# A decoder layer on one core: a third query ahead of the last quotients, half of one tile's scaling on VectorE, and the gate's second choice behind unit 4's scores

## The chip, the cores and the metric

The kernel runs on one core of one Trainium2 chip. The metric is the device time of one execution in microseconds (us). The engines are named as the profile names them: PE (TensorE, with its weight loads as PEld), DVE (VectorE), ACT (ScalarE), POOL (GpSimd) and SP (SyncE, which issues most transfers). SBUF is the on-chip memory, PSUM the accumulators, eight banks that the program calls `pb`.

## The reference

The input is `x`, 2 x 1024 tokens of 256 numbers, all float32. Three blocks are added to it in turn, each on its layer norm:

```
x = x + linear_attention(layernorm(x))      # k, q through elu+1, two decayed running sums, 16 heads, divided by q*running k
x = x + cross_attention(layernorm(x), ctx)  # 16 heads, 154 context rows per batch:
        att = softmax(where(mask, -inf, q k^T / 8 * side))
        out = (att v) Wo + bo
x = x + experts(layernorm(x))               # softmax gate over 8 experts, the best two per token,
        y = sum of the two experts' silu((x w1 + b1) * (x w3 + b3)) w2 + b2, weighted by their scores
        z = a shared expert of the same form; y + z is added
```

## The kernel before, in words

The 2048 tokens are 16 tiles of 128 tokens, four chunks `c` of four tiles, and eight units `u8` of two tiles. Each engine has its own program, written out by hand in one order; engines meet only in semaphores. A `Signal` is a semaphore with a list of events in order, `w.wait_ge(scaled.sem, scaled[t, hf])` waits for one of them.

The PSUM banks are given in rotation: `bank.take(key)` takes the next of the eight, `take_pair` two neighbours that one instruction of DVE will drain together (and it skips bank 7 when no pair fits). PE may fill a bank when its last user has drained it, `w.wait_ge(free[u.e], u.empty)`. So the order of the `take` calls on PE decides which earlier content each fill has to wait for.

First comes the linear attention, chunk by chunk. For chunk 3, PE makes the first queries of the cross attention for unit 0 (`queries(0, ...)`, L489, L498), the sum of the denominators (`densum`, L457), and after DVE's reciprocal (L1172) the spread quotients (`divided`, L468), which DVE multiplies in (L1180). The line `queries(0, range(4, 6))`, `divided(3)`, `queries(0, range(6, 8))` is L679 to L681.

Then the cross attention in units. For unit `u8` PE does the scores of two tiles in three groups of heads each (`scores`, L515), the queries of the next unit (L498), then for the unit before (`values`): the transposes of the softmax weights (`weights_turned`, L548; `hf` is a half of the 16 heads, `k` one bank of four transposes), the products with the values (`product`, L564 and L568), between them the place step of a gate (L623) in units 4 and 6 and the transposes of the next norm (`turned`, L394), then parts of the shared expert (L635, L647) and the combination with Wo (`combined`, L600, L612).

DVE, for each tile `t`: multiplies the scores with the side input (`scores`, L1206, three groups, draining the score banks), adds the mask (`mask`, L1217, two SBUF tensors), reduces to the maximum (`top`, L1224, L1227, L1230), takes the reciprocal of the softmax sum (`total`, L1236), and drains the value products (`product`, L1248) and the combination (`attended`, L1258). It also does norm statistics (`stats`, L1084, L1086), and for every second unit from 3 on the gate of a chunk: `logits`, then `gate`, in which each of some 20 steps (`step`, profiled as L1262) waits for the one before; after the first choice of an expert it calls `shared_act` (L1339), then makes the second choice. In unit 3 that is the gate of chunk 0. Its result, `gated[0]`, is used by PE's place step in unit 4.

ACT does the exponentials of the softmax (`exps`, L895), the evacuation of transposes and queries (L907, L886, L830) and the norms (L840). POOL multiplies the exponentials by the reciprocals into `wts` (`scale(t)`, L1668: for each half `hf` a product over the 26 context rows that exceed 128, L1680, 208 columns, and one over the first 128, L1682, 1024 columns), adds `boB` to x (`add_bo`, L1650, a product of 256 columns for each tile), computes the norms' roots (L1661 to L1666) and issues the scatters of tokens to their experts (L1686).

At the end come 36 slots of 128 rows, each with one expert's three matrices, and POOL adds their rows to the output in DRAM with indirect transfers (L1762).

Of the kernel before, what the change touches and what calls it, by code (L numbers as in the profile page):

```python
# [7 lines left out]
ALU = mybir.AluOpType  # L8
ACT = mybir.ActivationFunctionType
AX = mybir.AxisListType  # L10
# [5 lines left out]
P = 128  # L16
# [4 lines left out]
NT = N // P  # L21
NCH = 4
CT = 512
H = 16
# [147 lines left out]
def decoder(nc, A, xs, out):  # L172
    with ExitStack() as ctx:
# [6 lines left out]
        def signal(name, events):  # L180
            return Signal(sem(name), events)
# [166 lines left out]
        topped = signal("topped", [(t, hs, n) for t in range(NT) for hs in heads_of(t) for n in range(3)])  # L348
        raised = signal("raised", range(NT))
        summed = signal("summed", range(NT))  # L350
        scaled = signal("scaled", [(t, hf) for t in range(NT) for hf in range(2)])
        xbo = signal("xbo", range(NU))
        xsb = signal("xsb", range(NCH))
        gatexp = signal("gatexp", range(NCH))
# [26 lines left out]
        def _(e):  # L381
# [158 lines left out]
            def weights_turned(u8, hf, k):  # L540
                u = bank.take(("pT", u8, hf, k))
                w.wait_ge(free[u.e], u.empty)
                for i in range(2):
                    n = 2 * k + i
                    lo = P * (8 * hf + n) if n < 8 else 2048 + P * (2 * hf + n - 8)
                    for q in range(2):
                        w.wait_ge(scaled.sem, scaled[2 * u8 + q, hf])
                        ins = e.transpose(pb[:, u.i, (2 * i + q) * P:(2 * i + q + 1) * P], wts[q][:, lo:lo + P],  # L548
                                          ident[:, :])
                ins.then_inc(full[u.i], 1)  # L550
# [125 lines left out]
                    contents(b)  # L676
            queries(0, range(0, 4))
            densum(3)
            queries(0, range(4, 6))  # L679
            divided(3)  # L680
            queries(0, range(6, 8))  # L681
            scores(0)
            queries(1)
            mixed(3)
# [385 lines left out]
        def _(e):  # L1070
# [120 lines left out]
            def scores(t, groups=range(3)):  # L1191
                s = t % 2
                w.wait_ge(in_fs[s], 16 * (t // 2 + 1))
                if t < 3:
                    w.wait_ge(qkv.sem, qkv[3, 1])
                    d = bank["mix", 2 if t < 2 else 3, 1]
                    w.wait_ge(full[d.i], d.filled)
                else:
                    w.wait_ge(scaled.sem, scaled[t - 3, 1])
                for g in groups:  # L1200
                    lo, hi = TRIOS[g]
                    n = hi - lo
                    u, v = bank["s", t, g, 0], bank["s", t, g, 1]
                    w.wait_ge(full[u.i], u.filled)
                    w.wait_ge(full[v.i], v.filled)
                    e.tensor_tensor(  # L1206
                        att[t % 3][:, 2 * lo:2 * hi, :].rearrange("p (r h) k -> p r h k", r=2),
                        pb[:, u.i:u.i + 2, 0:n * SK].rearrange("p r (h k) -> p r h k", h=n),
                        fs[:, s, 2 * lo:2 * hi, :].rearrange("p (r h) k -> p r h k", r=2), ALU.mult
                    ).then_inc(free[u.i], 1)  # L1210
# [23 lines left out]
            def total(t):  # L1234
                w.wait_ge(raised.sem, raised[t])
                e.reciprocal(mx[:, t % 4, 3, :], mx[:, t % 4, 2, :]).then_inc(*summed.next(t))  # L1236

            def product(u8, hf):
                w.wait_ge(in_bv, 16)
# [29 lines left out]
            def gate(c, amid=None):  # L1269
                u = bank["gateT", c]  # L1270
                lg4 = pb[:, u.i, 0:P].rearrange("p (t n) -> p t n", t=4)[:, :, 0:NE]
                w.wait_ge(in_sm, 224)
                w.wait_ge(to_xs, 128 * sum(kc[0] == 3 for kc in NORMS[:NORMS.index((3, c)) - 1]))
                e.tensor_copy(xn[:, NORMS.index((3, c)) % 2, :, D].bitcast(I32), tokid[:, 4 * c:4 * c + 4]).then_inc(*chain.next())
                w.wait_ge(full[u.i], u.filled)
                step(e.tensor_reduce, gm[:, :], lg4, AX.X, ALU.max)
                w.wait_ge(chain.sem, chain.count)
                e.tensor_tensor(lg[:, :, :], lg4, per_token(gm[:, :]), ALU.subtract).then_inc(free[u.i], 1)
                w.wait_ge(gatexp.sem, gatexp[c])
                step(e.tensor_reduce, gm[:, :], lg[:, :, :], AX.X, ALU.add)  # L1280
                step(e.reciprocal, gm[:, :], gm[:, :])
                step(e.tensor_tensor, lg[:, :, :], lg[:, :, :], per_token(gm[:, :]), ALU.mult)
                step(e.tensor_tensor, ga[:, :, :], lg[:, :, :], per_expert(gbB[:, :]), ALU.add)
                if c:
                    w.wait_ge(second.sem, second[c - 1])
                for i, ox in enumerate((o1, o2)):
                    o = ox[:, 4 * c:4 * c + 4, :]
                    step(e.tensor_reduce, gm[:, :], ga[:, :, :], AX.X, ALU.max)
                    step(e.tensor_tensor, gt[:, :, :], ga[:, :, :], per_token(gm[:, :]), ALU.is_ge)
                    step(e.tensor_tensor, gt[:, :, :], gt[:, :, :], per_expert(iot[:, :]), ALU.mult)  # L1290
                    step(e.tensor_reduce, gm[:, :], gt[:, :, :], AX.X, ALU.max)
                    step(e.tensor_tensor, o, per_expert(iot[:, :]), per_token(gm[:, :]), ALU.is_equal)
                    step(e.tensor_tensor, gt[:, :, :], o, lg[:, :, :], ALU.mult)
                    step(e.tensor_reduce, wsel[:, i, :], gt[:, :, :], AX.X, ALU.add)
                    if i == 0:
                        step(e.scalar_tensor_tensor, out=ga[:, :, :], in0=o, scalar=-BIG, in1=ga[:, :, :],
                             op0=ALU.mult, op1=ALU.add)
                        if amid is not None:
                            amid()
                step(e.tensor_copy, xn[:, NORMS.index((3, c)) % 2, :, D + 1], wsel[:, 0, :])  # L1300
                w.wait_ge(chain.sem, chain.count)
                e.tensor_tensor(gt[:, :, :], o1[:, 4 * c:4 * c + 4, :], o2[:, 4 * c:4 * c + 4, :], ALU.add
                                ).then_inc(*gated.next(c))
# [98 lines left out]
            for u8 in range(1, NU):  # L1402
                t0, t1 = 2 * u8, 2 * u8 + 1
                gating = (u8 - 3) // 2 if u8 >= 3 and u8 % 2 else None
                if u8 == 7:
                    stats(3, 2, 2, 4)
                scores(t0)
                if u8 > 1:
                    total(t0 - 1)
                    scores(t1)  # L1410
                else:
                    stats(2, 2, 0, 2)
                    scores(t1, range(0, 2))
                    total(1)
                    scores(t1, range(2, 3))
                    stats(2, 2, 2, 4)
                if u8 == 4:
                    stats(2, 3)
                if gating is not None and u8 < 7:
                    stats(3, gating, 2, 4)  # L1420
                if u8 == 7:
                    shared_out(*FILL[6])
                for hs in heads_of(t0):
                    mask(t0, hs)
                for hs in heads_of(t0):
                    top(t0, hs)
                    if hs == (0, 8):
                        product(6, 0)
                mask(t1, (0, H))
                if u8 < 7:  # L1430
                    product(u8 - 1, 0)
                if u8 in (4, 6):
                    place(u8 // 2 - 2)
                if u8 < 7:
                    top(t1, (0, H))
                product(u8 - 1, 1)
                if gating is not None:
                    logits(gating)
                if u8 == 7:
                    top(t1, (0, H))  # L1440
                if u8 == 7:
                    shared_held(2, 0)
                total(t0)
                if u8 - 1 in FILL and u8 < 7:
                    shared_out(*FILL[u8 - 1])
                if gating is not None:
                    gate(gating, amid_gate if u8 == 7 else lambda: shared_act(*FILL[u8]))
                elif u8 in FILL:
                    shared_act(*FILL[u8])
                if u8 in (2, 4, 6):  # L1450
                    stats(3, u8 // 2 - 1, 0, 2)
                if u8 < 7:
                    attended(u8 - 1)
# [31 lines left out]
            shared_out(2, 1)  # L1485
            logits(3)
            gate(3, lambda: shared_act(3, 0))
            shared_act(3, 1)
            place(3)
            step(e.tensor_tensor, ntf[:, :], n_e, eoff[:, :], ALU.add)  # L1490
# [150 lines left out]
        def _(e):  # L1641
# [26 lines left out]
            def scale(t):  # L1668
# [5 lines left out]
                    w.wait_ge(full[d.i], d.filled)  # L1674
                main = wts[t % 2][:, 0:2048].rearrange("p (h k) -> p h k", h=H)
                rest = wts[t % 2][:, 2048:2560].rearrange("p (h k) -> p h k", h=H)
                for hf in range(2):
                    h8 = slice(8 * hf, 8 * hf + 8)
                    inv = mx[:, a4, 3, h8].rearrange("p (h a) -> p h a", a=1)
                    e.tensor_tensor(rest[:, h8, 0:SK - P], att[t % 3][:, h8, P:SK], inv.broadcast_to([P, 8, SK - P]),  # L1680
# [327 lines left out]
```

## Time and profile before

The median of three runs is 586.93 us (584.76 to 587.72).

| of the profiled execution | |
|---|---|
| its own time | 586.75 us |
| its span, first to last instruction | 584.8 us |
| PE busy | 563.0 us, 96% |
| PE weight loads | 426.4 us, 73% |
| DVE busy | 442.1 us, 76% |
| ACT busy | 325.1 us, 56% |
| POOL busy | 232.3 us, 40% |
| mean granted TensorE clock | 0.990 |

Busy time is what an engine spends in its instructions. A row of the timeline gives the start, the time from the start of the first to the end of the last instruction of the row, engine, line, operation, what it writes and reads, and the count; in square brackets stands idle time in front of it and what ended it. Consecutive instructions overlap a little, so starts tell more than durations. A row of the chain of waits gives start, duration and what ran.

### The profile page before, as it was taken

How to read it: one execution, taken by the hardware profiler on the slowest of the kernel's cores; microseconds unless marked ns; L12 is line 12 of the kernel's file. 1: busy time of each engine (PE TensorE's matmuls, PEld its weight loads, DVE VectorE, ACT ScalarE, POOL GpSimd, SP SyncE). 2: the span in 40 equal slices, each digit the busy share in tenths (PEclk: the TensorE clock that was granted, in tenths of full speed). 3: DMA queues.
4: the chain of work that ended last, by engine and by line, in shares of the span. 5: the costliest groups of instructions: out<-in, count | busy, mean ns of one | idle time of the engine just before them, and what ended most of it. 6: DMA issues, size and time to landing. Idle time of an engine off the chain costs nothing.

```text
span 584.8 us, 11124 instructions
## 1 busy us (share of the span) xinstructions
PE 563.0 (96%) x3656; PEld 426.4 (73%) x3656; DVE 442.1 (76%) x839; ACT 325.1 (56%) x1004; POOL 232.3 (40%) x228
## 2 busy tenths in 40 slices
PE   8999999999999999999999999999999999999980
PEld 6547566788797978789788887887777777667660
DVE  4999999999795979949688689867677556656650
ACT  3632424379869796895967939615223344555220
POOL 1010110307581834387243762635245343444443
PEclk9999999999999999999999999999999999999995
DMA  8920004162741321423215217892644434244323
GB/s 303 348 96 2 1 1 173 44 217 97 265 172 46 122 97 71 147 72 120 99 47 207 71 47 227 274 377 73 171 119 83 72 56 68 43 68 62 54 27 35
DMA packets 36183, 68.37 MB, mean 117 GB/s; under 512 B 5504, under 2 KB 29024, under 8 KB 33632
## 3 DMA queue, kind: packets, MB, share of 16 engines
q1 hardware_dynamic: 28208, 57.99, 29.7%
q0 software_dynamic: 6784, 8.95, 9.2%
q10 hardware_dynamic: 1136, 0.73, 0.4%
q8 instruction: 30, 0.49, 0.4%
q14 instruction: 25, 0.20, 0.1%
HBM read 56.62 MB, written 15.25 MB: 123 GB/s over the span
## 4 chain that ended last, share of the span: by engine, by line
PE 60%; DVE 17%; DMA 9%; issue 7%; POOL 3%; ACT 2%; POOLq 1%; SPq 0%; DVEq 0%
PE pb L743 9%; DMA out_dram<-R 6%; PE pb L635 6%; DVE R L1138 6%; PE pb L498 6%; PE pb L600 6%; PE pb L548 6%; PE pb L564 5%; PE pb L777 5%; PE pb L515 4%; PE pb L647 4%; DVE R L1161 3%; PE pb L612 2%; DMA out_dram<-R,hidx 2%; PE pb L568 2%
## 5 line engine op out<-in xcount | busy, mean ns | idle before, releaser
L895 ACT ACTIVATE R<-R,mx 128x154 f32<-128x154 f32 x256 | 104.4, 415 | 0.1
L1762 POOL DMA_INDIRECT out_dram<-R x36 | 55.6, 1546 | 83.0 <-DMA out_dram<-R 51.1
L743 PE MATMUL pb<-R 128*128 x256 | 81.0, 459 | 0.0
L1020 ACT ACTIVATE R<-R 128x352 f32<-128x352 f32 x36 | 17.9, 497 | 90.5 <-DVE R L1573 76.9
L743 PEld LDWEIGHTS pb<-R 128*128 128x128 f32 x256 | 46.2, 190 | 20.4
L498 PE MATMUL pb<-xnT,wq 128*128 128x256 f32 x256 | 58.2, 383 | 0.0
L886 ACT ACTIVATE R<-pb,bq 128x256 f32<-128x256 f32 x64 | 30.1, 473 | 48.0 <-PE pb L498 47.8
L498 PEld LDWEIGHTS pb<-xnT,wq 128*128 128x128 f32 x256 | 47.7, 190 | 7.8 <-issue 1.2
L907 ACT COPY R<-pb 128x512 f32<-128x512 f32 x80 | 40.8, 616 | 18.4 <-PE pb L548 18.3
L1686 POOL DMA_INDIRECT xs_dram<-xn,pos x32 | 31.9, 996 | 47.2 <-DVE pos L1322 38.9
L895 ACT ACTIVATION_READ_ACCUMULATOR R<-R,mx 128x1 f32 x256 | 49.4, 193 | 0.0
L1661 POOL TENSOR_TENSOR sd<-mv,cst 128x4 f32<-128x4 f32 x12 | 9.8, 814 | 98.1 <-DVE mv L1086 98.0
L1217 DVE SCALAR_TENSOR_TENSOR R<-R 128x2464 f32<-128x2464 uint8 (+1 forms) x18 | 48.7, 2710 | 0.0
L777 PE MATMUL pb<-R 128*128 (+1 forms) x192 | 47.1, 381 | 1.5 <-ACT R L1029 1.5
L1206 DVE TENSOR_TENSOR R<-pb,R 128x924 f32<-128x924 f32 (+1 forms) x48 | 45.2, 996 | 2.7 <-PE pb L515 2.7
L1224 DVE TENSOR_REDUCE mx<-R 128x16 f32<-128x2464 f32 (+1 forms) x18 | 43.7, 2428 | 0.3
L439 PE MATMUL pb<-xnT,R 128*128 128x512 f32 x96 | 43.0, 599 | 0.8 <-ACT xnT L830 0.8
L635 PE MATMUL pb<-xnT,sw 128*128 128x256 f32 (+1 forms) x192 | 43.4, 381 | 0.0
L600 PE MATMUL pb<-wo,R 128*128 128x256 f32 x192 | 42.5, 380 | 0.0
L600 PEld LDWEIGHTS pb<-wo,R 128*128 128x128 f32 x192 | 36.4, 190 | 5.4 <-issue 0.4
L635 PEld LDWEIGHTS pb<-xnT,sw 128*128 128x128 f32 (+1 forms) x192 | 34.2, 181 | 7.1 <-issue 0.8
L777 PEld LDWEIGHTS pb<-R 128*128 128x128 f32 (+1 forms) x192 | 34.0, 191 | 5.7 <-issue 2.4
(203 smaller groups left out, 1179.4 us busy)
## 6 DMA issues: line engine op xcount, KB each, us to landing
R<-in_fside_dram SPq DMA_DIRECT2D x16, 1232.0 KB, 5.6
R<-in_L_ffn_w_dram SPq DMA_DIRECT2D x16, 352.0 KB
R<-in_mask_dram SPq DMA_DIRECT2D x16, 308.0 KB, 2.9
R<-xs_dram SPq DMA_DIRECT2D x32, 129.0 KB, 2.1
KV<-in_ebias_dram SPq DMA_DIRECT2D x2, 1440.0 KB
out_dram<-x SPq DMA_DIRECT2D x4, 512.0 KB, 4.3
R<-in_L_ffn_w_dram SPq DMA_DIRECT2D x8, 256.0 KB, 4.4
x<-in_x_dram SPq DMA_DIRECT2D x3, 512.0 KB, 10.9
```

The costliest lines, as they stand in the source:

```text
L439: ins = e.matmul(pb[:, u.i, :], wqkv[:, k, col * P:(col + 1) * P], xnT[:, r, k, :], start=(k == 0), stop=(k == 1))
L498: ins = e.matmul(pb[:, u.i, 0:256], wq[:, k, j * P:(j + 1) * P], xnT[:, r, k, cols], start=(k == 0), stop=(k == 1))
L600: ins = e.matmul(pb[:, u.i, 0:D], oT[:, j, q * P:(q + 1) * P], wo[:, j, :], start=(j == 0), stop=(j == 7))
L635: ins = e.matmul(pb[0:mw, u.i, q * 256:q * 256 + 256], wm[:, k, lo:lo + mw], xnT[:, r, k, cols], start=(k == 0), stop=(k == 1))
L743: ins = e.matmul(pb[:, u.i, 0:F], xsT[:, s % 2, k, :], ew13[:, bass.ds(w_reg[s] * 1408 + q * 704 + k * F, F)], start=(k == 0), stop=(k == 1))
L777: ins = e.matmul(pb[:, u.i, 0:D], sT[0:mw, s % 2, m, :], ew2[0:mw, bass.ds(w_reg[s] * 768 + m * D, D)], start=(m == 0), stop=(m == 2))
L895: ins = e.activation(att[t % 3][:, h, :], att[t % 3][:, h, :], ACT.Exp, bias=mx[:, a4, 1, h:h + 1], accum_out=mx[:, a4, 2, h:h + 1])
L907: e.copy(pT[:, hf, 2 * k:2 * k + 2, :], pb[:, u.i, :].rearrange("p (i q) -> p i q", i=2)).then_inc(free[u.i], 1)
L1206: e.tensor_tensor(att[t % 3][:, 2 * lo:2 * hi, :].rearrange("p (r h) k -> p r h k", r=2), pb[:, u.i:u.i + 2, 0:n * SK].rearrange("p r (h k ...
L1217: e.scalar_tensor_tensor(out=att[t % 3][:, lo:hi, :], in0=mk[:, s, lo:hi, :], scalar=-BIG, in1=att[t % 3][:, lo:hi, :], op0=ALU.mult, op1= ...
L1224: e.tensor_reduce(mx[:, a4, 0, lo:hi], att[t % 3][:, lo:hi, :], AX.X, ALU.max).then_inc(*topped.next((t, hs, 0)))
L1762: e.indirect_dma_start(out=out, out_offset=bass.IndirectOffsetOnAxis(ap=to.bitcast(U32), axis=0), in_=rows, in_offset=None, compute_op=ALU ...
```

## The change

On PE, the queries of unit 0 for head pair 6 are issued ahead of `divided(3)` and not behind it. On DVE and POOL, the second half (heads 8 to 15) of tile 1's scaling moves from POOL's `scale(1)` to a new function `scale_half` on DVE, called behind tile 3's last score group and ahead of the last two statistics of norm (2, 2). It has a signal of its own, `halved`, for which PE waits in the transposes of that half and DVE in the scores of tile 4. The gate's loop over the two choices becomes a function `choice(c, i)`; `second_choice(c)` holds the second with the two steps behind it. It is called right behind `gate` as before for chunks 1, 2 and 3; for chunk 0 it is called in unit 4, behind `scores(9)`, and no longer in unit 3.

```
-        scaled = signal("scaled", [(t, hf) for t in range(NT) for hf in range(2)])
+        scaled = signal("scaled", [(t, hf) for t in range(NT) for hf in range(2) if (t, hf) != (1, 1)])
+        halved = signal("halved", [0])
...
                     for q in range(2):
-                        w.wait_ge(scaled.sem, scaled[2 * u8 + q, hf])
+                        if (2 * u8 + q, hf) == (1, 1):
+                            w.wait_ge(halved.sem, halved[0])
+                        else:
+                            w.wait_ge(scaled.sem, scaled[2 * u8 + q, hf])
...
             densum(3)
-            queries(0, range(4, 6))
+            queries(0, range(4, 7))
             divided(3)
-            queries(0, range(6, 8))
+            queries(0, range(7, 8))
...
-                    w.wait_ge(scaled.sem, scaled[t - 3, 1])
+                    w.wait_ge(scaled.sem, scaled[t - 3, 0 if t == 4 else 1])
+                    if t == 4:
+                        w.wait_ge(halved.sem, halved[0])
...
+            def scale_half():
+                w.wait_ge(summed.sem, summed[1])
+                w.wait_ge(zeroed.sem, zeroed["pad1"])
+                h8 = slice(8, H)
+                main = wts[1][:, 0:2048].rearrange("p (h k) -> p h k", h=H)
+                rest = wts[1][:, 2048:2560].rearrange("p (h k) -> p h k", h=H)
+                inv = mx[:, 1, 3, h8].rearrange("p (h a) -> p h a", a=1)
+                e.tensor_tensor(rest[:, h8, 0:SK - P], att[1][:, h8, P:SK], inv.broadcast_to([P, 8, SK - P]), ALU.mult)
+                e.tensor_tensor(main[:, h8, :], att[1][:, h8, 0:P], inv.broadcast_to([P, 8, P]), ALU.mult
+                                ).then_inc(*halved.next(0))
...
-                for i, ox in enumerate((o1, o2)):
-                    o = ox[:, 4 * c:4 * c + 4, :]
-                    step(e.tensor_reduce, gm[:, :], ga[:, :, :], AX.X, ALU.max)
...
+                choice(c, 0)
+                if amid is not None:
+                    amid()
+
+            def choice(c, i):
+                o = (o1, o2)[i][:, 4 * c:4 * c + 4, :]
+                step(e.tensor_reduce, gm[:, :], ga[:, :, :], AX.X, ALU.max)
+                step(e.tensor_tensor, gt[:, :, :], ga[:, :, :], per_token(gm[:, :]), ALU.is_ge)
+                step(e.tensor_tensor, gt[:, :, :], gt[:, :, :], per_expert(iot[:, :]), ALU.mult)
+                step(e.tensor_reduce, gm[:, :], gt[:, :, :], AX.X, ALU.max)
+                step(e.tensor_tensor, o, per_expert(iot[:, :]), per_token(gm[:, :]), ALU.is_equal)
+                step(e.tensor_tensor, gt[:, :, :], o, lg[:, :, :], ALU.mult)
+                step(e.tensor_reduce, wsel[:, i, :], gt[:, :, :], AX.X, ALU.add)
...
+            def second_choice(c):
+                choice(c, 1)
                 step(e.tensor_copy, xn[:, NORMS.index((3, c)) % 2, :, D + 1], wsel[:, 0, :])
                 w.wait_ge(chain.sem, chain.count)
                 e.tensor_tensor(gt[:, :, :], o1[:, 4 * c:4 * c + 4, :], o2[:, 4 * c:4 * c + 4, :], ALU.add
...
                 if u8 > 1:
                     total(t0 - 1)
                     scores(t1)
+                    if u8 == 4:
+                        second_choice(0)
                 else:
                     stats(2, 2, 0, 2)
                     scores(t1, range(0, 2))
                     total(1)
                     scores(t1, range(2, 3))
+                    scale_half()
                     stats(2, 2, 2, 4)
...
                 if gating is not None:
                     gate(gating, amid_gate if u8 == 7 else lambda: shared_act(*FILL[u8]))
+                    if u8 != 3:
+                        second_choice(gating)
...
-                for hf in range(2):
+                for hf in range(1 if t == 1 else 2):
```

## Rows read from the trace of the kernel before

**Rows 1.** Waits of PE over the whole span: total us, times, longest us.

```profile
PE pb L548 <- POOL R L1682: 0.8, 1, 0.8
...
PE pb L515 <- DVE R L1206: 0.7, 2, 0.6
```

**Rows 2.** Chain of waits, expert stage: start us, us, what.

```profile
516.14 4.32 DMA out_dram<-R
```

**Rows 3.** Timeline of PE and its weight loads, units 0 and 1.

```profile
106.61 1.99 PE L498 MATMUL pb<-xnT,wq 128*128 128x256 f32 x8
...
109.34 1.17 PE L468 MATMUL pb<-R,hZ 32*128 32x128 f32 x32 [0.73 <-DVE R L1172]
...
112.36 4.68 PE L515 MATMUL pb<-KV,R 64*128 64x154 f32 x64
...
138.19 4.18 PEld L498 LDWEIGHTS pb<-xnT,wq 128*128 128x128 f32 x20 [0.34 <-DVE R L1206]
...
146.75 0.33 PE L548 MATMUL pb<-ident,R 128*128 128x128 f32 x1 [0.82 <-POOL R L1682]
...
151.62 1.95 PE L564 MATMUL pb<-R,KV 128*64 128x256 f32 x16
```

**Rows 4.** Timeline of DVE, units 0 and 1.

```profile
109.20 2.29 DVE L1161 TENSOR_TENSOR R<-R 128x1024 f32<-128x1024 f32 x2
...
113.92 5.60 DVE L1206 TENSOR_TENSOR R<-pb,R 128x924 f32<-128x924 f32 x6
...
139.96 0.41 DVE L1084 BATCH_NORM_STATS2 st<-x 128x6 f32<-128x256 f32 x1
...
141.04 3.41 DVE L1217 SCALAR_TENSOR_TENSOR R<-R 128x2464 f32<-128x2464 uint8 x1
...
144.48 2.72 DVE L1224 TENSOR_REDUCE mx<-R 128x16 f32<-128x2464 f32 x1
...
147.45 0.67 DVE L1230 SCALAR_TENSOR_TENSOR mx<-mx 128x16 f32<-128x16 f32 x1
...
148.04 3.31 DVE L1217 SCALAR_TENSOR_TENSOR R<-R 128x2464 f32<-128x2464 uint8 x1
...
151.28 1.27 DVE L1248 TENSOR_TENSOR R<-pb,bvT 128x512 f32<-128x512 f32 x2
```

**Rows 5.** Timeline of POOL, unit 1.

```profile
139.96 1.90 POOL L1682 TENSOR_TENSOR R<-R,mx 128x1024 f32<-128x1024 f32 x1
...
141.82 3.02 POOL L1680 TENSOR_TENSOR R<-R,mx 128x208 f32<-128x208 f32 x1
...
144.80 1.89 POOL L1682 TENSOR_TENSOR R<-R,mx 128x1024 f32<-128x1024 f32 x1
...
146.66 5.30 POOL L1650 TENSOR_TENSOR x<-x,boB 128x256 f32<-128x256 f32 x4
```

**Rows 6.** Timeline of PE, units 4 and 5.

```profile
225.06 2.69 PE L515 MATMUL pb<-KV,R 64*128 64x154 f32 x32
...
228.31 2.52 PE L515 MATMUL pb<-KV,R 64*128 64x154 f32 x32 [0.56 <-DVE R L1206]
...
245.23 1.04 PE L394 MATMUL pb<-ident,xn 128*128 128x128 f32 x8
...
263.57 4.47 PE L515 MATMUL pb<-KV,R 64*128 64x154 f32 x64
```

**Rows 7.** Timeline of DVE, the gate in unit 3, units 4 and 5.

```profile
220.49 1.60 DVE L1262 TENSOR_TENSOR gt<-ga,gm 128x32 f32<-128x32 f32 x1
...
222.12 0.19 DVE L1262 TENSOR_TENSOR gt<-gt,iot 128x32 f32<-128x32 f32 x1
...
224.53 0.17 DVE L1262 TENSOR_REDUCE gm<-ga 128x4 f32<-128x32 f32 x1
...
226.28 0.19 DVE L1302 TENSOR_TENSOR gt<-o 128x32 f32<-128x32 f32 x1
...
227.06 2.84 DVE L1206 TENSOR_TENSOR R<-pb,R 128x924 f32<-128x924 f32 x3
...
232.69 0.41 DVE L1084 BATCH_NORM_STATS2 st<-x 128x6 f32<-128x256 f32 x1
...
240.62 2.72 DVE L1217 SCALAR_TENSOR_TENSOR R<-R 128x2464 f32<-128x2464 uint8 x1
...
244.06 1.29 DVE L1248 TENSOR_TENSOR R<-pb,bvT 128x512 f32<-128x512 f32 x2 [0.72 <-PE pb L568]
...
264.83 2.85 DVE L1206 TENSOR_TENSOR R<-pb,R 128x924 f32<-128x924 f32 x3 [0.72 <-PE pb L515]
```

**Rows 8.** Timeline of POOL, scaling of tile 7.

```profile
232.98 1.90 POOL L1682 TENSOR_TENSOR R<-R,mx 128x1024 f32<-128x1024 f32 x1
```

More of the change, by code:

```diff
@@ L1285, in gate @@
                     w.wait_ge(second.sem, second[c - 1])
-                for i, ox in enumerate((o1, o2)):
-                    o = ox[:, 4 * c:4 * c + 4, :]
-                    step(e.tensor_reduce, gm[:, :], ga[:, :, :], AX.X, ALU.max)
[L1289 to L1299, printed above, removed]
+                choice(c, 0)
[10 more added lines that the diff above has]
+                step(e.tensor_reduce, wsel[:, i, :], gt[:, :, :], AX.X, ALU.add)
+                if i == 0:
+                    step(e.scalar_tensor_tensor, out=ga[:, :, :], in0=o, scalar=-BIG, in1=ga[:, :, :],
+                         op0=ALU.mult, op1=ALU.add)
+            def second_choice(c):
+                choice(c, 1)
                 step(e.tensor_copy, xn[:, NORMS.index((3, c)) % 2, :, D + 1], wsel[:, 0, :])
@@ L1487, in _ @@
             gate(3, lambda: shared_act(3, 0))
+            second_choice(3)
             shared_act(3, 1)
```

## The prediction

> **What bounds the kernel now.** I read the waits of PE first. They are few: the three that the edits aim at are 0.8 us for POOL's L1682, 0.7 for DVE's score products [rows 1] and 0.73 for its reciprocal [rows 3], so even with every one of them gone the kernel could win some 2 to 3 us of 587. The chain of waits then says what the end depends on: in the attention units it is a string of PE pieces, and from about 516 us on it is the scatter-adds of the last slots, which follow PE's expert stage [rows 2]. So a microsecond that PE loses or wins in a unit moves the end by as much, unless something later was waiting for another engine anyway. The reader is to see that the question is not PE's work, which does not change by one instruction, but when VectorE (DVE) frees PSUM banks. The timelines of the three engines around units 0, 1 and 4 show that.
>
> How DVE and GpSimd (POOL) disturb each other decides two of the three edits. POOL's 208-column product of L1680 took 3.02 us beside DVE's mask, which is more than its 1024-column one (1.90); and DVE's mask (2.7 us undisturbed, by its ends) took 3.41 and 3.31 us when POOL was in the middle of an operation [rows 4, 5]. In the gate a 32-column DVE product took 1.60 us, while POOL scaled, and the other small ones 0.17 to 0.2 [rows 7]. I read: one waits until the other's instruction has ended; at each such end the one that waited comes next, so they alternate. DVE operations with PSUM as a source, reductions and statistics ran beside POOL at their usual length.
>
> The Trainium skill, SBUF — State Buffer, section Who interferes with whom, says the same in general: a VectorE instruction with two SBUF inputs and a GpSimd one that reads SBUF exclude each other for a whole instruction. Its page Perfetto Trace Analysis, section Optimizing Scalar/DVE Operations, warns that moving work between these two may therefore not help, which speaks against the second edit; by a reading without that exclusion the sum would be 585.0 us, with it 589.6. The trace agrees with the exclusion, by the rows of 3.02 and 1.60 us.
>
> **Part 1, a third query ahead of the quotients.** No instruction is added. PE waited 0.73 us for the reciprocal before its 32 quotient matmuls at 109.34; two queries took 106.61 to about 108.34, so one takes 0.87 us and a third ends at 109.2, just in the gap [rows 3]. Those quotients feed DVE's L1180, which could only start at 111.5, behind two products from 109.20 of 2.29 us [rows 4]; so nothing on DVE moves. After the reordering one quotient bank less lies ahead of the first score groups and one more behind; DVE frees the last at about 113.9, where its score products start [rows 4]; the pair that now takes it is the first of tile 1, which PE, with its scores 0.75 us earlier than 112.36 and 2.2 us for a tile, reaches at 113.8 [rows 3]: at worst 0.1 us. But DVE works without a gap from 109 to 151 [rows 4] and PE waits for it again: its weights of unit 2's third query were loaded at 138.19 only when DVE had freed the bank of tile 3's first group [rows 3]. That time is DVE's, which this edit does not change, so the gain is eaten there. Bounds: -0.7 us (were it kept) to +0.1; I take 0, which the row at 138.19 supports.
>
> **Part 2, DVE scales half of tile 1.** Removed: POOL's second pair on tile 1, 208 and 1024 columns, which ran 141.82 to 146.7; PE's transpose that should have come at 145.77 came at 146.75 [rows 3, 5]. Gain if nothing else is late: 0.98 us. Added on DVE before tile 2's mask: the same two products. Not in this trace on DVE; the nearest row is L1161, 1024 columns in 1.15 us, so 1.1 and 0.25, together 1.35 us without a wait. With waits:
> - the last score product lets DVE go at about 139.96, exactly where POOL's L1682 of the first half starts [rows 5]. This is a tie. I take it that POOL is first, since DVE's instruction has two semaphores ahead of it: DVE waits until 141.82, and its small product ends at 142.1;
> - POOL's additions of boB (four, each 0.7 us: 5.30 less the 2.5 that they stood behind the mask) now begin at 141.82 [rows 5]. The first comes between: to 142.8. DVE's large product ends at 143.9;
> - the two statistics take 1.08 us as before, to 145.0; the third addition holds the mask to 145.3. It ended 2.6 us after POOL had let go (144.45 against 141.82), so 147.9;
> - reduction and one small operation 3.0 us as before (to 147.45), so 150.9, the second small one 0.1 (it took 0.67 when POOL disturbed it; POOL is done), then tile 3's mask without a wait, 2.65, to 153.65; the first L1248 frees its banks 0.63 later, 154.3. Before it was 151.28 + 0.63 = 151.9 [rows 4].
>
> So DVE is 2.4 us late. Who waits? PE's second product of unit 0 starts at 151.62; its fifth head (0.235 us each, 1.88 over 8) writes into the bank that the first product's first pair has left, at 152.56 [rows 3]. It was 0.6 us behind the release; now it comes at 154.34: +1.78 us, and the 0.98 is lost in front of it. ScalarE's two exponentials before its last evacuations also start later, at about 151.1, but these end by 153.1 and stay hidden. The combination after it needs DVE's second L1248, at about 158.8, for matmuls that PE then reaches at 159.6: hidden. Were DVE first at 139.96, its small product is through at 140.2, POOL's L1682 to 142.1, the large one to 143.2, and mask and release are 0.7 us earlier: +1.1 us. Without any exclusion the delay is 1.35 us less the about 2.0 that POOL's longer work cost DVE before (0.8, 0.5 and 0.7), so PE keeps its 0.98. Bounds -1.0 and +1.8; I take +1.8.
>
> **Part 3, the gate's second choice after unit 4's scores.** Nine small DVE instructions move, 224.53 to 226.4, some 0.22 us apart, 1.9 us [rows 7]. Behind them lay attended(2) and scores(8); PE's tile 8 took 2.69 us for 32 matmuls and tile 9 started at 228.31, where undisturbed 64 take 4.47 us [rows 6], so that it could have started at 227.26. Now the residual addition waits for PE's last combination at 225.1, and the first score product can start as in unit 5, 1.26 us behind PE's first score, at 226.3 instead of 227.06 [rows 6, 7]. The bank that tile 9's first group shares with tile 8's first is free at 227.5 (a group takes 0.95, and 0.15 to PE): PE wins 0.8 us there. DVE ends its scores 0.75 us earlier too, at 231.95 (statistics began at 232.69). Then the choice meets POOL's scaling of tile 7, also 0.75 earlier, whose last L1682 would run 232.2 to 234.1 [rows 7, 8]: one product slips in at the boundary, the next waits for its end, seven more take 1.3 us, so that the statistics start at 235.4, 2.7 us late. From that start to the end of tile 9's mask it was 10.65 us (244.06 less 0.72 idle), so it ends at 246.05, and the first L1248 frees its banks at 246.7. PE's second transpose of the next norm (the second half of its row at 245.23, so 245.67) goes into the first of them; PE would be there at 244.85. It comes at 246.75: +1.08 us against before, and the 0.8 is lost. The place step of the gate follows the same L1248 and is 2.0 us late; POOL's scatters and then its scaling of tile 8 with it, which has about 1.7 us to spare before DVE needs it. The choice's result is there at 235.4, 8 us ahead of PE's use. Bounds: -0.9 (no wait for POOL, no bank late) and +1.8 (scores(8) not earlier, all of DVE 0.75 later); I take +1.1.
>
> **Sum.** 0 + 1.78 + 1.08 = 2.86 on the profiled execution's 586.75 us (span 584.8 and 1.95 around it): 589.6 us. Against the median of the runs shown, 586.93, that is 2.7 us or 0.46% more; the three runs lie 3 us apart. What this measurement tells from no change is 0.5%, 2.9 us, so the forecast itself is mostly within it.
>
> **Rivals.**
> - Faster: POOL and DVE hardly disturb each other in the new places, or DVE's late banks have more room than I count. Then PE keeps 1.0 in unit 1 and 0.8 in unit 4: 585.0 us, 584.3 if part 1's 0.7 were kept too. For it: in the rows PE's listed waits really sit on these releases. Against it: the rows of 3.02 and 1.60 us [rows 5, 7].
> - One of the two pays: unit 1 costs 1.8 and unit 4 wins 0.8, 587.7 us; or unit 1 wins 1.0 and unit 4 costs 1.1, 586.9. For it: unit 4 has 0.72 us of DVE idle in front of the bank [rows 7], unit 1 none.
> - Clearly slower: in unit 4 scores(8) starts no earlier than 227.06, because the release of its banks and not the choice held it. Then the choice ends 0.75 us later, tile 9's mask with it, and PE stands at the transpose until 247.5: +1.8 there, +1.8 in unit 1, 590.4 us. It decides from the point where DVE starts scores(8) later than about 226.6. Against it: the 1.26 us of unit 5.
>
> **Chances.** Forecast 0.50, with 588.8 to 590.3 as its own range; faster rival 0.18; one of the two 0.18; clearly slower 0.12; rest 0.02. A third of the forecast (it reaches past 589.9) and most of the last case are slower by over 0.5%: 0.27. Faster by over 0.5% needs under 584.0: 0.04. Within 0.5%: 0.69. The range: from the faster rival, 585.0, to 590.8, the slower one with some spread.
>
> **What would show it.** Part 1: no wait at L468, PE's first scores about 0.75 us earlier, and a longer wait for L1206 around 138. Part 2: no wait of L548 on POOL; DVE's new small product of up to 2 us; a new wait of PE at L564 on L1248 near 154. Part 3: tile 9 starts under 0.4 us late; one choice instruction of about 1.8 us; a wait at L394 on L1248 near 246 plus the shift. Wrong if the choice's instructions all take 0.2 us, or if L564 and L394 don't wait.

## The result, and the profile after

The changed kernel takes 588.75 us (median of 13 runs, 587.43 to 590.21) against 585.94 us for the kernel before (13 runs on the same chip, 584.76 to 587.81). The ratio is 1.0043, its 95% interval 1.0031 to 1.0054, so about 2.5 us are lost, between 1.8 and 3.2. The profiled execution took 590.06 us, its span 588.3. Two runs of e1_query below (656.67 and 1184.69 us) and one of the kernel before (1503.13 us) were slow ones and count in no median or ratio.

Single times differ by 2 to 3 us from run to run, as much as the loss itself. So I read the loss inside the span too, as a **distance on PE's timeline**: from the start of unit 1's scores (L515 before, L516 after) to the first matmul of the expert stage (L743 before, L747 after). It leaves out the start and the tail of scatter-adds, where most of the spread lies: over the ten profiles of this document the time from that first expert matmul to the end varies from 170.2 to 173.4 us, with the same instructions in it. Before, it runs from 131.86 to 412.32, 280.46 us; after, from 132.10 to 414.93, 282.83 us: 2.37 us longer. The profiled span grew by more than that, 3.5 us; the kernel before itself spans 172.5 us from that first expert matmul on, the changed one 173.4. The distance starts behind the place of part 1, so part 1 needs a stretch of its own: from the first matmul of the query row at 101.92 (102.29 after) to the scores of unit 1 it is 29.94 us before and 29.81 after, 0.13 us less. From there to the expert stage the change costs 2.24 us.

The busy times, from the first part of the page, say little: PE does the same instructions, DVE two more, POOL two fewer.

```profile
PE 563.2 (96%) x3656; PEld 426.0 (72%) x3656; DVE 445.8 (76%) x841; ACT 325.5 (55%) x1004; POOL 228.7 (39%) x226
```

PE's waits over the whole span (total us, times, longest us) say it at once. POOL's 0.8 us of [rows 1] is gone and the 0.7 us for score products has shrunk to 0.2. Two new waits stand there, both for DVE's L1265, the eviction of the value products (L1248 in the prediction):

```profile
PE pb L568 <- DVE R L1265: 1.8, 1, 1.8
...
PE pb L395 <- DVE R L1265: 1.6, 1, 1.6
...
PE pb L516 <- DVE R L1212: 0.2, 1, 0.2
```

PE's timeline of units 0 and 1 (start us, us; in brackets the idle time and its releaser) answers [rows 3]. The third query fills the gap at 109.8, and the scores behind it start earlier by 0.66 us against scores(1) but take 5.35 us instead of 4.68. The second value product of unit 0, one run before, now breaks at its fifth head, as forecast:

```profile
106.99 2.86 PE L499 MATMUL pb<-xnT,wq 128*128 128x256 f32 x12
109.77 1.18 PE L469 MATMUL pb<-R,hZ 32*128 32x128 f32 x32
...
111.94 5.35 PE L516 MATMUL pb<-KV,R 64*128 64x154 f32 x64
...
132.10 4.47 PE L516 MATMUL pb<-KV,R 64*128 64x154 f32 x64
...
150.87 1.08 PE L568 MATMUL pb<-R,KV 128*64 128x256 f32 x8
153.73 1.08 PE L568 MATMUL pb<-R,KV 128*64 128x256 f32 x8 [1.78 <-DVE R L1265]
```

DVE's timeline of the same stretch answers [rows 4]. Its second new product holds 1024 columns and occupies DVE for 2.92 us; what that time is made of shows only beside POOL's row of 140.21:

```profile
140.20 0.36 DVE L1251 TENSOR_TENSOR R<-R,mx 128x208 f32<-128x208 f32 x1
140.48 2.92 DVE L1252 TENSOR_TENSOR R<-R,mx 128x1024 f32<-128x1024 f32 x1
...
144.40 2.87 DVE L1223 SCALAR_TENSOR_TENSOR R<-R 128x2464 f32<-128x2464 uint8 x1
...
153.00 1.28 DVE L1265 TENSOR_TENSOR R<-pb,bvT 128x512 f32<-128x512 f32 x2
```

POOL's timeline there, against [rows 5]: one pair for tile 1 instead of two, then the four additions, now 6.27 us.

```profile
140.21 2.11 POOL L1710 TENSOR_TENSOR R<-R,mx 128x1024 f32<-128x1024 f32 x1
142.28 6.27 POOL L1678 TENSOR_TENSOR x<-x,boB 128x256 f32<-128x256 f32 x4
```

Units 4 and 5 on PE answer [rows 6]: tile 9's scores come 2.53 us behind tile 8's (3.25 before), and then the transposes, one row of eight before, stand 1.65 us in their middle.

```profile
226.31 2.37 PE L516 MATMUL pb<-KV,R 64*128 64x154 f32 x32
228.84 2.52 PE L516 MATMUL pb<-KV,R 64*128 64x154 f32 x32 [0.15 <-DVE R L1212]
...
245.75 0.60 PE L395 MATMUL pb<-ident,xn 128*128 128x128 f32 x4
248.00 0.65 PE L395 MATMUL pb<-ident,xn 128*128 128x128 f32 x4 [1.65 <-DVE R L1265]
```

The gate's second choice on DVE answers [rows 7], and POOL's scaling of tile 7 [rows 8]. One of the nine small instructions takes 1.81 us, and it ends with POOL's product, at 235.4:

```profile
233.41 0.19 DVE L1279 TENSOR_TENSOR gt<-ga,gm 128x32 f32<-128x32 f32 x1
233.64 1.81 DVE L1279 TENSOR_TENSOR gt<-gt,iot 128x32 f32<-128x32 f32 x1
235.48 0.19 DVE L1279 TENSOR_REDUCE gm<-gt 128x4 f32<-128x32 f32 x1
...
247.26 1.28 DVE L1265 TENSOR_TENSOR R<-pb,bvT 128x512 f32<-128x512 f32 x2
```

```profile
233.50 1.90 POOL L1710 TENSOR_TENSOR R<-R,mx 128x1024 f32<-128x1024 f32 x1
```

### The profile page after: what moved, and what is told of

Read it like the earlier page. It is cut to its first block, busy times and chain, and to the rows that moved or that the text cites. A ratio compares the mean times of both kernels' runs of the same rounds, so it can differ in the third digit from the quotient of the medians.

```text
span 588.3 us, 11124 instructions
## 1 busy us (share of the span) xinstructions
PE 563.2 (96%) x3656; PEld 426.0 (72%) x3656; DVE 445.8 (76%) x841; ACT 325.5 (55%) x1004; POOL 228.7 (39%) x226
## 4 chain that ended last, share of the span: by engine, by line
PE 56%; DVE 22%; DMA 9%; issue 8%; POOL 2%; POOLq 1%; ACT 1%; DVEq 0%; SPq 0%
PE pb L747 7%; PE pb L639 7%; PE pb L604 7%; DMA out_dram<-R 6%; DVE R L1142 6%; PE pb L499 5%; PE pb L552 5%; PE pb L568 4%; PE pb L516 4%; PE pb L781 4%; PE pb L651 3%; DVE R L1165 3%; PE pb L616 2%; DMA out_dram<-R,hidx 2%; DVE st L1088 2%
## 5 line engine op out<-in xcount | busy, mean ns | idle before, releaser
L747 PE MATMUL pb<-R 128*128 x256 | 81.0, 460 | 0.0
L747 PEld LDWEIGHTS pb<-R 128*128 128x128 f32 x256 | 46.2, 190 | 20.3
```

Source lines behind the costliest of these rows:

```text
L747: ins = e.matmul(pb[:, u.i, 0:F], xsT[:, s % 2, k, :], ew13[:, bass.ds(w_reg[s] * 1408 + q * 704 + k * F, F)], start=(k == 0), stop=(k == 1))
```

## The experiments

The theory: part 1 is worth next to nothing, parts 2 and 3 each cost about 1 us, in each case because DVE, which works in order, reaches the eviction L1265 later, and part of that lateness is POOL's operation that DVE has to wait out. The rivals: the loss is DVE's added or moved work alone, whatever POOL does; or it is one part's; or a spread of the whole over the run. Each kernel was timed in several rounds beside the kernel before. "Distance" is the one defined above, with its difference from the 280.46 us before; "by unit 7" is the part of that difference that stands at the start of unit 7's scores (206.12 us behind scores(1) before). scores(1) is the start of unit 1's scores.

| kernel | median us (runs) | ratio to before, 95% | distance us | difference | by unit 7 |
|---|---|---|---|---|---|
| after | 588.75 (13) | 1.0043, 1.0031 to 1.0054 | 282.83 | +2.37 | +2.14 |
| e1_query | 585.81 (10) | 0.9998, 0.9984 to 1.0012 | 280.46 | 0.00 | +0.01 |
| e2_half | 587.76 (12) | 1.0032, 1.0015 to 1.0050 | 281.70 | +1.24 | +0.99 |
| e3_choice | 587.42 (12) | 1.0029, 1.0013 to 1.0046 | 281.59 | +1.13 | +1.14 |
| e4_choice_late | 585.94 (12) | 0.9998, 0.9984 to 1.0013 | 279.98 | -0.48 | -0.49 |
| e5_half_none | 585.03 (10) | 0.9993, 0.9983 to 1.0003 | 279.41 | -1.05 | -1.03 |
| e6_half_twice | 589.48 (4) | 1.0072, 1.0053 to 1.0091 | 284.87 | +4.41 | +4.32 |
| e7_half_free | 585.32 (10) | 0.9997, 0.9985 to 1.0010 | 280.45 | -0.01 | -0.17 |
| e8_both_late | 585.14 (12) | 0.9997, 0.9988 to 1.0007 | 279.97 | -0.49 | -0.48 |

The kernel before had 585.82 us beside the first four experiments and 585.26 beside the last four. Each distance comes from one profiled execution. The diffs below show a part of each edit, marked where they are taken against another run than the kernel before.

**e1_query: part 1 alone.**

```diff
-            queries(0, range(4, 6))
+            queries(0, range(4, 7))
             divided(3)
-            queries(0, range(6, 8))
+            queries(0, range(7, 8))
```

> Part 1 alone: query 6 of unit 0 ahead of the last quotients. Theory (PE's gain is eaten by DVE's late release of a score bank): no wait of PE for the reciprocal, PE's first scores 0.75 us earlier, but the weights of unit 2's third query load at the same time as before (about 138.2), time within 0.2 us of the kernel before. Rival (the gain is kept): -0.7 us.

Measured: a distance of 280.46 us, that of before to the last digit, and a ratio of 0.9998. The distance begins behind the edit, so it only says that nothing later moved, and the interval of the ratio (0.9984 to 1.0012) is too wide to exclude the rival's 0.7 us. The rows ahead of scores(1) decide: from the query row at 102.23 (101.92 before) to scores(1) it is 29.79 us against 29.94. The wait at L468 is gone, and 0.15 us came of it. PE's timeline shows where the rest went: unit 0's scores, 4.68 us before, take 5.34.

```profile
106.92 2.86 PE L498 MATMUL pb<-xnT,wq 128*128 128x256 f32 x12
109.70 1.17 PE L468 MATMUL pb<-R,hZ 32*128 32x128 f32 x32
...
111.87 5.34 PE L515 MATMUL pb<-KV,R 64*128 64x154 f32 x64
```

They start 20.15 us ahead of scores(1) (at 132.02), against 19.50 before: 0.65 us earlier, and 0.66 us longer. PE's weight loads, one row without a break before, pause three times in them, for 0.34, 0.18 and 0.20 us; the last two pauses end with DVE's L1206, for the first the profile names no releaser.

**e2_half: part 2 alone.**

```diff
                     scores(t1, range(2, 3))
+                    scale_half()
                     stats(2, 2, 2, 4)
...
-                for hf in range(2):
+                for hf in range(1 if t == 1 else 2):
```

> Part 2 alone: DVE scales half of tile 1. Theory (DVE's large product waits for POOL's, and with it the release of the first value product's banks): a wait of PE of about 1.8 us in the second value product, PE 1.0 us late at the combination of unit 0, time +1.0 us. Rival (the part's gain of 0.98 us is real and part 3 alone costs): -0.8 to -1.0 us.

Measured: +1.24 us by the distance, and 0.9 to 2.9 us by the times. The wait in front of the fifth head is there. DVE's product is as long as in the full change, PE's wait 1.82 us against 1.78:

```profile
140.17 2.92 DVE L1252 TENSOR_TENSOR R<-R,mx 128x1024 f32<-128x1024 f32 x1
```

```profile
153.41 1.08 PE L568 MATMUL pb<-R,KV 128*64 128x256 f32 x8 [1.82 <-DVE R L1265]
...
155.05 7.17 PE L616 MATMUL pb<-wo,R 128*128 128x256 f32 x32
```

Unit 0's combination (L616) starts 23.26 us behind scores(1), against 22.25 before: +1.01 us. At the scores of units 5, 6 and 7 the shift is +1.00, +0.99 and +0.99 us. Of the last 0.24 us, 0.20 come at the last transposes of a norm (L395 at 396.53): PE stands 0.40 us in front of them and not 0.20, since DVE's norm (L1100) had waited 0.26 us for a scatter transfer. The same 0.20 us is there in the full change and in e7_half_free, and not in e6_half_twice, which has part 2 as well. So it isn't DVE's added work in unit 1, and part 2 as such costs 1.0 us; why the transfer was late in three profiles isn't shown.

**e3_choice: part 3 alone**, `second_choice(0)` directly behind unit 4's `scores(t1)`.

```diff
                     scores(t1)
+                    if u8 == 4:
+                        second_choice(0)
```

> Part 3 alone: the second choice of chunk 0 behind unit 4's scores. Theory: tile 9's scores 0.7 us earlier, one choice instruction of 1.8 us beside POOL's scaling, a wait of PE of about 1.65 us at the transposes of the next norm, +1.1 us in all. Rival (it gains the scores' wait and the rest is hidden): -0.7 us.

Measured: +1.13 us by the distance, +1.15 already at unit 5's scores; by the times 0.8 to 2.7 us. DVE's rows show the choice caught once, PE's waits in 105 to 330 us the price:

```profile
232.48 0.19 DVE L1273 TENSOR_TENSOR gt<-ga,gm 128x32 f32<-128x32 f32 x1
232.70 1.82 DVE L1273 TENSOR_TENSOR gt<-gt,iot 128x32 f32<-128x32 f32 x1
```

```profile
PE pb L394 <- DVE R L1259: 1.7, 1, 1.7
PE pb L548 <- POOL R L1703: 0.8, 1, 0.8
```

The three parts add up: 0 + 1.24 + 1.13 = 2.37 us, the whole, and by unit 7 0.01 + 0.99 + 1.14 = 2.14, the whole again. So no part disturbs another, and all but 0.24 us of the loss arises in units 1 and 4.

**e4_choice_late: part 3 with the choice between tile 8's reduction and tile 9's mask**, where POOL is idle. The DVE work ahead of the eviction is the same as in e3_choice.

```diff
+                if u8 == 4:
+                    second_choice(0)
                 mask(t1, (0, H))
```

> Part 3 with the second choice between the maxima of tile 8 and the mask of tile 9, where POOL is idle: the same nine instructions ahead of the same bank release, without POOL beside them. Theory (of the 2.7 us by which the release is late, 1.6 is POOL's): no choice instruction over 0.25 us, a wait at the transposes of about 0.2 us, tile 9's scores 0.7 us earlier as in part 3, time -0.5 us. Rival (it is DVE's added work, wherever it stands, that makes the bank late): +0.5 to +1.1 us.

Measured: -0.48 us by the distance. All nine instructions take 0.2 us or less; the product that took 1.82 us is the second of these:

```profile
240.31 0.19 DVE L1273 TENSOR_TENSOR gt<-ga,gm 128x32 f32<-128x32 f32 x1
240.53 0.19 DVE L1273 TENSOR_TENSOR gt<-gt,iot 128x32 f32<-128x32 f32 x1
...
244.60 1.28 DVE L1259 TENSOR_TENSOR R<-pb,bvT 128x512 f32<-128x512 f32 x2
```

and PE passes the transposes in one row, with no wait listed. The row takes 1.28 us instead of 1.04, and by these 0.24 us the 0.72 won at tile 9's scores shrinks to 0.48:

```profile
244.71 1.28 PE L394 MATMUL pb<-ident,xn 128*128 128x128 f32 x8
```

Counted from scores(1) (132.07 here, 132.18 in e3_choice, where the eviction starts at 246.34), the eviction starts 1.63 us earlier, exactly what the choice's product is shorter. So the sign of part 3 is POOL's doing: the same work without POOL beside it turns +1.13 into -0.48. The ratio of 0.9998 can't tell a gain of 0.5 us from none; its interval only just meets that of e3_choice, at 1.0013.

**e5_half_none: the second half of tile 1 is scaled by neither engine** (PE waits for the first half's signal instead). It shows what removing POOL's pair would bring if DVE did nothing in its place.

```diff
-                    scale_half()
```

(against e2_half)

> Part 2 with the scaling of tile 1's second half left out altogether, on POOL and on DVE (the transposes read what lies there, so that half of tile 1's output is wrong). Theory (the part fails by what it adds on DVE, not on POOL or PE): no wait of PE on POOL nor for the value product's banks, the combination of unit 0 0.9 to 1.0 us earlier than in the kernel before, time -1.0 us. Rival (PE cannot use the 0.98 us, since the banks are late even without added work): the combination no earlier than 0.3 us before, time -0.3 us or more.

Measured: -1.05 us by the distance. Unit 0's combination comes 1.03 us earlier, and there is no break in the value product; in DVE's rows tile 2's mask is as long as before (3.41 us), and the eviction starts 18.31 us behind scores(1) (at 132.05), 2.59 us earlier than in the full change (20.90):

```profile
141.22 3.41 DVE L1218 SCALAR_TENSOR_TENSOR R<-R 128x2464 f32<-128x2464 uint8 x1
...
150.36 1.28 DVE L1260 TENSOR_TENSOR R<-pb,bvT 128x512 f32<-128x512 f32 x2
```

```profile
150.78 1.95 PE L565 MATMUL pb<-R,KV 128*64 128x256 f32 x16
```

So part 2 does remove a wait of PE worth 1.0 us, and DVE's half costs 0.99 + 1.03 = 2.02 us by unit 7.

**e6_half_twice: part 2 alone, with DVE's large product done twice.**

```diff
+                w.wait_ge(halved.sem, halved[0])
+                e.tensor_tensor(main[:, h8, :], att[1][:, h8, 0:P], inv.broadcast_to([P, 8, P]), ALU.mult
+                                ).then_inc(*halved.next(1))
```

(against e2_half)

> Part 2 with DVE's product of 1024 columns done twice, one after the other. Theory (every microsecond on DVE ahead of this bank release is one on PE): the second costs its 1.1 us and up to 0.7 us behind one of POOL's additions, PE's expert stage 1.1 to 1.8 us later than with part 2 alone, time +2.1 to +3.0 us against the kernel before. Rival (the loss is a fixed change of order): as part 2 alone, +1.2 us.

Measured: +4.41 us by the distance and 1.0072 by the times, more than I expected. DVE's extra product took 1.65 us (the first one 2.92 again), and the eviction starts at 154.38:

```profile
140.18 2.92 DVE L1252 TENSOR_TENSOR R<-R,mx 128x1024 f32<-128x1024 f32 x1
143.14 1.65 DVE L1255 TENSOR_TENSOR R<-R,mx 128x1024 f32<-128x1024 f32 x1
...
154.38 1.28 DVE L1268 TENSOR_TENSOR R<-pb,bvT 128x512 f32<-128x512 f32 x2
```

```profile
155.12 1.08 PE L568 MATMUL pb<-R,KV 128*64 128x256 f32 x8 [3.50 <-DVE R L1268]
156.13 1.16 PE L572 MATMUL pb<-R,KV 32*64 32x256 f32 x16
157.21 8.33 PE L616 MATMUL pb<-wo,R 128*128 128x256 f32 x32
```

PE's wait grew from 1.82 to 3.50 us, by the 1.69 us that DVE is later. That is the price the theory names, one for one. The rest is another thing, and no wait for a bank: the products L572 behind it took 1.16 us instead of 0.69 and the combination 8.33 instead of 7.17, while DVE's second eviction (158.62 to 159.90) was over before PE came to its heads. The granted TensorE clock was 1.00 up to 156.1, 0.50 (1.2 GHz, half of 2.4) from 156.2 to 159.4, and 1.00 again from 159.6 on; the combination's first five matmuls start 0.43 us apart and the later ones 0.22. It fell after PE had stood 3.50 us, and in none of these profiles does it fall in this stretch after the waits of 1.82 us and less. So of the 3.33 us by which this run exceeds e2_half by unit 7, 1.68 are the wait and 0.47 + 1.16 = 1.63 the slower clock.

**e7_half_free: part 2 alone, with POOL's 1024-column product of tile 1's first half left out**. DVE's work is that of e2_half.

```diff
+                    if t == 1:
+                        e.memset(main[:, 0, 0:8], 0.0).then_inc(*scaled.next((t, hf)))
+                        continue
```

(against e2_half; the memset of 8 columns stands in the product's place and carries its signal)

> Part 2 with POOL's product of 1024 columns of tile 1's first half left out (that quarter of unit 0's weights is not scaled, so its output is wrong), so that DVE's products find POOL only at its additions of 0.7 us. Theory (DVE's 1.35 us of work is nearly repaid by what POOL no longer takes from DVE; the loss is the 1.8 us behind POOL's large product): DVE's large product under 1.9 us, the combination of unit 0 within 0.3 us of the kernel before, expert stage 1.0 to 1.4 us earlier than with part 2 alone. Rival (the added work itself is the loss): at most 0.5 us earlier than with part 2 alone.

Measured: -0.01 us by the distance, 1.25 us less than e2_half, -0.17 by unit 7, and a ratio of 0.9997, whose interval (0.9985 to 1.0010) doesn't meet that of e2_half (1.0015 to 1.0050). DVE's product took 1.75 us instead of 2.92, and PE's wait is 0.64 us:

```profile
141.73 1.75 DVE L1252 TENSOR_TENSOR R<-R,mx 128x1024 f32<-128x1024 f32 x1
```

```profile
153.80 1.08 PE L568 MATMUL pb<-R,KV 128*64 128x256 f32 x8 [0.64 <-DVE R L1265]
```

PE reaches its fifth head's bank at the same point in both: the row in front starts 18.72 us behind scores(1) in each (152.07 and 150.51), so the whole difference is the wait. By the rival, DVE's work alone, it should have cost what e2_half costs. That one is out.

**e8_both_late: part 1, no part 2, and the second choice of chunks 0 and 1 late**, in units 4 and 6, as a version that might beat both kernels.

```diff
+                if u8 in (4, 6):
+                    second_choice(u8 // 2 - 2)
                 mask(t1, (0, H))
```

> A candidate: part 1, no part 2, and the second choice of chunk 0 and of chunk 1 between the maxima and the second mask of units 4 and 6. Theory: -0.5 us in unit 4 as in the run with the late choice; in unit 6 PE lost 0.42 us in its scores to the choice before them, DVE idled 2.5 us ahead of the same bank release, so the choice is hidden there: -0.4 us more, expert stage 0.9 us earlier, time -0.9 us. Rival (another wait replaces it in unit 6): -0.5 us.

Measured: -0.49 us by the distance, no more than e4_choice_late (and 0.12 us ahead of scores(1), as part 1 gives); the ratio, 0.9997, isn't distinguishable from 1. The 0.4 us expected of unit 6 did not come: tile 13's scores start 2.52 us behind tile 12's, and before it was the same (301.22 and 303.74).

```profile
301.30 2.37 PE L515 MATMUL pb<-KV,R 64*128 64x154 f32 x32
303.82 2.37 PE L515 MATMUL pb<-KV,R 64*128 64x154 f32 x32
306.12 7.17 PE L498 MATMUL pb<-xnT,wq 128*128 128x256 f32 x32
```

```profile
302.55 2.85 DVE L1206 TENSOR_TENSOR R<-pb,R 128x924 f32<-128x924 f32 x3 [0.72 <-PE pb L515]
```

DVE only became more idle ahead of these scores (0.72 us, 0.53 before): its products start 1.25 us behind PE's first score, with the choice in front of them or not, so PE and not the choice sets their start. It beats the changed kernel (588.75) by about 2.7 us (0.9997 against 1.0043), and the kernel before by nothing that can be told.

## Why the prediction was right

The forecast was 589.6 us, with the prediction's own range for it from 588.8 to 590.3; measured were 588.75, just below that and well inside 585.0 to 590.8. Of the 0.85 us between them 0.8 is the starting point: the sum was added to one execution of 586.75 us, and the median of 13 is 585.94. The sum of the parts was 2.86 us. The ratio says 2.5, with 1.8 to 3.2, and the stretches on PE's timeline 2.37 - 0.13 = 2.24 us; that the two medians lie 2.81 us apart, almost the sum, is luck.

**Part 1, 0 us: right, for a reason only nearly right.** 0.15 us was won in e1_query and 0.13 in the full change. The wait at L468 went and DVE ate nearly all of the gain. But I put the place at the third query of unit 2, near 138, where PE's weight load now waits 0.39 us instead of 0.34. It is earlier: the scores of unit 0 lost 0.66 us themselves, in the stretch where I had costed a late bank at 0.1. The argument "DVE is busy without a gap, so it is DVE's time" gave the number; the bank by bank count did not.

**Part 2, +1.78 us: right in mechanism and place, too large.** The removed 0.98 us is real (1.03 in e5_half_none). The new wait is at the fifth head, for the first L1265, and the delayed eviction is what PE waits for. The term that was mis-sized is the tie at 139.96: I took POOL first, with +1.1 us as the other case, and it was the other case. In the full change and in e2_half and e6_half_twice DVE's 208-column product got in first (0.36 us, at 140.20 in the full change), POOL's large one took 2.11 or 2.12 instead of 1.90, and the eviction came at 153.0, its release at 153.64; that is 21.54 us behind scores(1). I had 154.3 for POOL first and 153.6 for DVE first; measured from the same start (131.86) it is 153.4. Unit 0's combination was +1.02 us late in the full change. With +1.1 in its place the sum would have been 2.2 us. A further 0.24 us comes after unit 7 and was in no step; 0.20 of it is the transfer that DVE waited for, described under e2_half.

**Part 3, +1.08 us: right in each step.** Tile 9 wins 0.72 us (forecast 0.8). Of the nine instructions one takes 1.81 us, until POOL's L1710 ends at 235.4. All of unit 4 is 1.25 us later there than before (226.31 against 225.06), so in before's time that is 234.15, forecast 234.1. The transposes wait 1.65 us in their middle for L1265 and go on at 248.00, in before's time 246.75, the forecast to the digit. Net 1.13 us. It held also that the later result of the gate costs nothing: the choice is through at 236.8, and no wait for it is listed.

**The rivals.** Faster (585.0 us) supposed little disturbance between POOL and DVE. e7_half_free and e4_choice_late are what it would have looked like: without POOL's large product beside it, part 2 costs nothing and part 3 gains 0.48. "One of the two pays" is out, as each costs. Clearly slower (590.4) turned on DVE starting tile 8's score products later than about 226.6 in before's time. In the full change it starts at 227.57 with all of unit 4 1.25 us later (226.31 against 225.06), so at 226.32 in before's time; in e3_choice, where nothing else is moved, at 226.64 with unit 4 0.32 us later, again 226.32. The forecast had 226.3.

**What the runs leave open**: why DVE waited for a transfer at the last norm in three of the profiles (0.20 us), and whether a gain of 0.5 to 1.0 us ahead of the expert stage (e4, e5, e8) reaches the end, since the ratios of those three don't stand out from 1.

## What to carry to other kernels

A wait that an engine has for one resource can go and leave the time as it was or longer: follow the engine that now does the work to the next buffer that it frees, and ask how far behind that release its next user stands. In unit 1 that was 0.6 us, and the edit delayed the release by more than this and what it had won together. Work moved to DVE or along its order is to be priced with the POOL instruction that runs at its new place, by start and end of both: it made 2.92 us of an estimated 1.1 and 1.81 us of 0.2, and a place one step further on, with POOL idle, turned the third edit's loss into a small gain. Where an effect is as large as the spread of single runs, a distance between two fixed points on the bounding engine's timeline settles in one profile what the times only hint at, as long as the edit lies between the two points: part 1's 0.15 us lay outside and needed a stretch of its own.

## What the runs showed of the hardware

- **In a near tie a small DVE product got past POOL.** Where DVE's 208-column product and POOL's 1024-column one started within 0.01 us of each other (140.20 and 140.21; the same in e2_half and e6_half_twice), DVE's took 0.36 us and POOL's 2.11 instead of 1.90 us. POOL lost 0.2 us by it; DVE's next product, begun 0.3 us later, took 2.92 us, 1.8 more than the estimated 1.1.
- **The waiting engine came next at a boundary.** POOL's product ended at 142.32 and DVE's 1024-column one at 143.40, 1.08 us later, with POOL's first addition behind it. That DVE product took 2.92 us in all, 1.75 us where only one addition of boB (about 0.7 us) was in its way, and its repetition 1.65 us between additions. Free of POOL it would be about 1.1, by the prediction's estimate; no run shows it alone. The Trainium skill, SBUF — State Buffer, section Who interferes with whom, has the exclusion for whole instructions, and these rows agree; what each engine waits shows as busy time and as no wait in any view.
- **TensorE's clock fell once behind a wait.** In e6_half_twice PE stood 3.50 us for a bank, and from 156.2 to 159.4 the granted clock was 0.50, 1.2 GHz. It made 1.63 us more of the matmuls behind, in rows that name no wait. Behind waits of 1.82, 1.78 and 1.66 us it stayed at 1.00. So the price of a delay isn't constant: 1.7 us more on DVE cost PE 3.3 us.
